# A third spread inflow (chunk 8) and six rows of C streamed through three tiles in a two-direction state-space kernel

## The reference

```
delta = softplus(dlt @ Wdt.T + bdt)              # per channel and token
for n in range(16):                              # N states of a channel
    h_n[t] = exp(delta[t] * A_n) * h_n[t-1] + delta[t] * B[t, n] * u[t]
y[t] = sum_n h_n[t] * C[t, n]  (+ u[t] * Dp)
```

## Time and profile before

| | us |
|---|---|
| median of 3 runs (lowest to highest) | 3288.13 (3287.22 to 3289.47) |
| the profiled execution | 3287.01 |
| its span, first to last instruction | 3285.2 |
| PE busy (share) | 2993.0 (91%) |
| DVE busy | 3017.2 (92%) |
| ACT busy | 2678.5 (82%) |
| POOL busy | 2903.7 (88%) |
| DMA moved | 560.40 MB, mean 171 GB/s |

### The profile page before, as it was taken

How to read it: one execution, slowest core, us unless ns; L and a number is a source line. 1 busy time by engine, 2 the same in 40 slices (tenths; PEclk the granted TensorE clock), 3 DMA queues, 4 the chain that set the end, 5 groups by cost and what they waited for, 6 DMA issues and landing times.

```text
span 3285.2 us, 54883 instructions
## 1 busy us (share of the span) xinstructions
PE 2993.0 (91%) x19924; PEld 2375.2 (72%) x19924; DVE 3017.2 (92%) x2008; ACT 2678.5 (82%) x5151; POOL 2903.7 (88%) x1288
## 2 busy tenths in 40 slices
PE   8887999899998999899999999899998999899999
PEld 5765666677677666678877767678777666677789
DVE  2838999999999999999999999999998999999994
ACT  1448999988888999987788999987877999988772
POOL 1528999999999999999999999999998999999993
PEclk9989999999999999999999999999999999999999
DMA  5775334644476333645465334645566343645463
GB/s 224 236 244 171 136 117 137 227 154 163 162 248 207 130 123 131 228 144 163 159 243 192 130 123 134 224 139 165 165 217 207 120 132 130 232 136 163 156 198 111
DMA packets 207053, 560.40 MB, mean 171 GB/s; under 512 B 20200, under 2 KB 66472, under 8 KB 202560
## 3 DMA queue, kind: packets, MB, share of 16 engines
q1 hardware_dynamic: 203424, 538.01, 48.5%
q0 software_dynamic: 2304, 16.78, 1.3%
q10 hardware_dynamic: 1056, 2.10, 0.2%
HBM read 476.19 MB, written 80.63 MB: 169 GB/s over the span
## 4 chain that ended last, share of the span: by engine, by line
PE 49%; ACT 20%; DVE 12%; issue 10%; POOL 1%; DVEq 0%; ACTq 0%; POOLq 0%
PE y L888 14%; PE slot L899 10%; PE mb L859 9%; ACT abuf L1134 8%; PE mb L969 6%; DVE hbuf L1326 6%; ACT slot L1195 3%; DVE hbuf L1335 3%; PE mb L869 3%; PE slot L911 3%; DVE slot L1326 3%; ACT dec L1195 2%; PE mb L930 1%; ACT soft L1090 1%; ACT yrd L1125 1%
## 5 line engine op out<-in xcount | busy, mean ns | idle before, releaser
L1239 POOL TENSOR_TENSOR hbuf<-hbuf,cres 128x1024 f32<-128x1024 f32 x704 | 1664.4, 2377 | 143.9 <-DVE hbuf L1326 143.8
L1234 POOL TENSOR_TENSOR bst<-bst,du 128x1024 f32<-128x1024 f32 x512 | 1220.2, 2383 | 46.7 <-DVE du L1270 46.7
L1326 DVE TENSOR_TENSOR_SCAN hbuf<-dec,slot 128x1024 f32<-128x1024 f32 x512 | 1165.0, 2275 | 40.3 <-PE slot L911 27.2
L888 PE MATMUL y<-ident,hbuf 128*128 128x128 f32 x8192 | 1016.0, 273 | 1.8 <-POOL hbuf L1239 1.7
L888 PEld LDWEIGHTS y<-ident,hbuf 128*128 128x128 f32 x8192 | 923.9, 141 | 106.4 <-issue 103.5
L1134 ACT ACTIVATE abuf<-dut,bt 128x128 f32<-128x128 f32 x3072 | 964.7, 387 | 0.0
L1326 DVE TENSOR_TENSOR_SCAN slot<-slot,bst 128x1024 f32<-128x1024 f32 x320 | 728.3, 2276 | 22.5 <-ACT slot L1195 22.1
L1195 ACT ACTIVATE slot<-delta,par 128x1024 f32<-128x1024 f32 x512 | 568.4, 1110 | 199.6 <-DVE hbuf L1335 186.6
L1195 ACT ACTIVATE dec<-delta,par 128x1024 f32<-128x1024 f32 x512 | 584.2, 1141 | 118.7 <-DVE hbuf L1326 118.1
L899 PE MATMUL slot<-ident,abuf 128*128 128x128 f32 x3072 | 408.6, 276 | 170.8 <-ACT abuf L1134 160.1
L899 PEld LDWEIGHTS slot<-ident,abuf 128*128 128x128 f32 x3072 | 339.0, 141 | 303.4 <-ACT abuf L1134 243.0
(11 more groups left out here) (157 smaller groups left out, 2301.3 us busy)
## 6 DMA issues: line engine op xcount, KB each, us to landing
bst<-bc_s SPq DMA_DIRECT2D x512, 512.0 KB, 3.9
cres<-bc_s SPq DMA_DIRECT2D x128, 512.0 KB, 6.8
wzs<-wz_s SPq DMA_DIRECT2D x64, 256.0 KB, 4.0
yf_s<-yrd SPq DMA_DIRECT2D x32, 512.0 KB, 5.3
ybuf<-yf_s SPq DMA_DIRECT2D x32, 512.0 KB, 4.8
yg_s<-ybuf SPq DMA_DIRECT2D x31, 512.0 KB, 4.4
si_s<-silu SPq DMA_DIRECT2D x28, 512.0 KB, 6.1
silu<-si_s SPq DMA_DIRECT2D x28, 512.0 KB, 5.4
```

What stands on the lines that cost most here:

```text
L888: last = nc.tensor.matmul(y[:, j * P:(j + 1) * P], hbuf[:, q % HR, j * P:(j + 1) * P], ident[:], start=False, stop=(q % N == N - 1), is_tr ...
L1234: nc.gpsimd.tensor_tensor(bst[:, i % BR, :], bst[:, i % BR, :], du[:, k % 2, :], ALU.mult).then_inc(pool_b, 1)
L1239: nc.gpsimd.tensor_tensor(hbuf[:, q % HR, :], hbuf[:, q % HR, :], cres[:, q % N, :], ALU.mult).then_inc(pool_prod, 1)
L1326: nc.vector.tensor_tensor_scan(h[:, ::step], decays[:, ::step], inflows[:, ::step], 0.0, ALU.mult, ALU.add).then_inc(scanned, 1)
```

## The change

`KINDS[8]` goes from A to E: chunk 8 becomes spread. Its two `scale_half` calls (chunks 6 and 7) go; the two of chunk 10 move from chunks 8 and 9 to 7 and 8. A third set of diagonals is made: before the first unit, and at chunk 3 of the first unit of every later group. `cres` shrinks from 16 tiles to 13: ten rows of C stay loaded for a group, and the six of `STREAMED` go through a ring of three tiles and are loaded anew in every unit, each when the product three streamed rows before it is done. `dec` gets a ring size, which is 1.

```diff
-KINDS = "EVAVEVAPAVAPAPAV"
-SCALE_STEPS = {0: ((2, 0), (2, 1)), 3: ((6, 0),), 5: ((6, 1),), 6: ((8, 0),), 7: ((8, 1),), 8: ((10, 0),),
-               9: ((10, 1),), 10: ((12, 0),), 11: ((12, 1),), 12: ((14, 0),), 13: ((14, 1),)}
+KINDS = "EVAVEVAPEVAPAPAV"
+SCALE_STEPS = {0: ((2, 0), (2, 1)), 3: ((6, 0),), 5: ((6, 1),), 7: ((10, 0),), 8: ((10, 1),),
+               10: ((12, 0),), 11: ((12, 1),), 12: ((14, 0),), 13: ((14, 1),)}
...
+STREAMED = (0, 3, 5, 8, 11, 13)
+KEPT = [n for n in range(N) if n not in STREAMED]
+CR = 3
+DECS = 1
...
+STREAM = [q for q in range(NU * N) if q % N in STREAMED]
...
-        cres = sb("cres", [P, N, S])
+        cres = sb("cres", [P, len(KEPT) + CR, S])
...
+            def load_streamed(i):
+                q = STREAM[i]
+                g = q // SEQ
+                sp.dma_start(cres[:, len(KEPT) + i % CR, :],
+                             scratch["bc"][g % 2, g // 2, N + q % N, :].partition_broadcast(P)).then_inc(cs_in[i % CR], 16)
...
-            for n in range(3):
+            load_streamed(0)
+            for n in (1, 2):
                 load_c(0, n)
+            for i in range(1, CR):
+                load_streamed(i)
...
                         load_b(before("VP", q - 2) + BR)
-                    if k == 0 and c + 3 < N:
+                    if k == 0 and c + 3 in KEPT:
                         load_c(0, c + 3)
+                    if q >= 5 and (q - 5) % N in STREAMED and stream_index(q - 5) + CR < len(STREAM):
+                        wait_product(sp, q - 5)
+                        load_streamed(stream_index(q - 5) + CR)
...
-                        wait_product(sp, q - ET)
+                        wait_product(sp, N * k + KEPT[c - ET])
...
-                    if e == ET - 1 and k + 1 < NU and c >= 5:
+                    if e == ET - 1 and k + 1 < NU and c - 5 in KEPT:
                         wait_product(sp, q - 5)
                         load_c(k // ET + 1, c - 5)
-                    if e == 0 and k >= ET and c < 5:
+                    if e == 0 and k >= ET and c < 5 and N - 5 + c in KEPT:
                         wait_product(sp, q - 5)
                         load_c(k // ET, N - 5 + c)
...
             make_diagonal(0, 1)
+            make_diagonal(0, 2)
...
-                        if before("AE", q) > 0:
-                            act.wait_ge(scanned, TURNED[before("AE", q) - 1] + 1)
-                        decays = dec[:]
+                        if before("AE", q) >= DECS:
+                            act.wait_ge(scanned, TURNED[before("AE", q) - DECS] + 1)
+                        decays = dec[:, before("AE", q) % DECS, :]
...
-                    if c == 1 and k > 0 and k % ET == 0:
-                        make_diagonal(k // ET, 1)
+                    if c in (1, 3) and k > 0 and k % ET == 0:
+                        make_diagonal(k // ET, (c + 1) // 2)
```

More of the change, by code:

```diff
@@ L537, in ssm_kernel @@
         delta, du = (sb(n, [P, 2, S]) for n in ("delta", "du"))
-        soft, ud, yrd, silu, ybuf, dec, dut = (sb(n, [P, S]) for n in (
-            "soft", "ud", "yrd", "silu", "ybuf", "dec", "dut"))
+        soft, ud, yrd, silu, ybuf, dut = (sb(n, [P, S]) for n in (
+            "soft", "ud", "yrd", "silu", "ybuf", "dut"))
+        dec = sb("dec", [P, DECS, S])
         abuf = sb("abuf", [P, 2, S])
@@ L554, in ssm_kernel @@
         c_in = [sem(f"c_in{n}") for n in range(N)]
+        cs_in = [sem(f"cs_in{i}") for i in range(CR)]
         last_in = sem("last_in")
@@ L617, in z_bank, with stream_index, c_tile, wait_c @@
             return mb[h] if k > 0 else y[:, half(h)]
+        def stream_index(q):
+            return q // N * len(STREAMED) + STREAMED.index(q % N)
+        def c_tile(q):
+            if q % N in STREAMED:
+                return cres[:, len(KEPT) + stream_index(q) % CR, :]
+            return cres[:, KEPT.index(q % N), :]
+        def wait_c(eng, q):
+            if q % N in STREAMED:
+                eng.wait_ge(cs_in[stream_index(q) % CR], 16 * (stream_index(q) // CR + 1))
+            else:
+                eng.wait_ge(c_in[q % N], 16 * (q // SEQ + 1))
         def wait_scanned_out(eng, q):
@@ L694, in load_c @@
             def load_c(g, n):
-                sp.dma_start(cres[:, n, :],
+                sp.dma_start(cres[:, KEPT.index(n), :],
                              scratch["bc"][g % 2, g // 2, N + n, :].partition_broadcast(P)).then_inc(c_in[n], 16)
+            def load_streamed(i):
[3 more added lines that the diff above has]
+                             scratch["bc"][g % 2, g // 2, N + q % N, :].partition_broadcast(P)).then_inc(cs_in[i % CR], 16)
             def load_forward_y(k):
@@ L1236, in product @@
             def product(q):
-                pool.wait_ge(c_in[q % N], 16 * (q // SEQ + 1))
+                wait_c(pool, q)
                 pool.wait_ge(scanned, q + 1)
-                nc.gpsimd.tensor_tensor(hbuf[:, q % HR, :], hbuf[:, q % HR, :], cres[:, q % N, :],
+                nc.gpsimd.tensor_tensor(hbuf[:, q % HR, :], hbuf[:, q % HR, :], c_tile(q),
                                         ALU.mult).then_inc(pool_prod, 1)
@@ L1318, in _ @@
                         dve.wait_ge(turned, before("AE", q + 1))
-                        decays, inflows = dec, slot[q % 2]
+                        decays, inflows = dec[:, before("AE", q) % DECS, :], slot[q % 2]
                     else:
@@ L1333, in _ @@
                         dve.wait_ge(scanned, q + 1)
-                        dve.wait_ge(c_in[c], 16 * (q // SEQ + 1))
-                        nc.vector.tensor_tensor(hbuf[:, q % HR, :], slot[q % 2][:], cres[:, c, :],
+                        wait_c(dve, q)
+                        nc.vector.tensor_tensor(hbuf[:, q % HR, :], slot[q % 2][:], c_tile(q),
                                                 ALU.mult).then_inc(dve_prod, 1)
```

## The result

The changed kernel takes **3366.20 us** (median of four runs, 3361.04 to 3372.34), against 3287.68 (3284.75 to 3289.47) for the kernel before on the same chip: a ratio of 1.0241, with a 95% interval of 1.0229 to 1.0253. The forecast was 3349 us, slower; the sign and the range hold, and the size is 17 us short. The profiled execution is 3369.61 us, 82.6 us above that of before.

What follows compares the result with a forecast made beforehand. DVE was taken as the bound nearly everywhere, with PE a second bound in series in silu units. Terms 26 + 2 + 10 + 22 = 60 us on 3287.0 gave 3347, as a median about 3349 us; range 3317 to 3379.

Steps and rivals of the forecast that it cites:

- the spread, PE later in 32 silu units: Chunk 8's spread makes PE 0.82 us later; DVE waits 0.8 us at the next chunk 0: 26 us.
- diagonals at seven group starts: At chunk 3 of seven later units the set delays decays: 3 x 2.0 + 4 x 1.0 = 10 us.
- before the first scan and in the first unit: Before the first unit the set of diagonals stands straight before the decay DVE awaits: 2.4 us.
- streamed row ahead of the tile: At chunk 13 of gate units with a block the tile lands 1.25 us later, DVE loses 0.9: 22 us.
- gate units without a projection, the tail: PE pauses in gate units take up most of the spread's delay; tail loads are used late: both 0.
- The wait at chunk 5: At group starts DVE waits 2 us for the decay of chunk 5; a sign to show in the profile after.
- the rival of the lower clock level: Tile waits about 1.9 us more, or the projection runs at lower clock after PE's pause: 3390 us, chance 0.07.
- The rows themselves: The six streamed rows of C arrive in time for their products; no POOL or DVE wait: 0.
- The clock: Rival that replacing eight transposes with true matmuls raises PE's clock, gaining 27 us: 3322 us, chance 0.02.
- ACT's relief: Removing ACT's scaling of chunk 8, some 2.5 us of a unit, gains 0.

Runs made afterwards that it cites:

- the half spread: Changed kernel with only four of the eight blocks of chunk 8's inflow made: 3334.33 us, ratio 1.0147.
- moving the set: Changed kernel with the third set of diagonals of later groups made at chunk 6 instead of chunk 3: 3349.51 us, ratio 1.0189.
- the z shift: Kernel before with the next unit's projection z in parts of 3, 2, 2, 1 instead of 2, 2, 2, 2, except in gate units: 3283.94 us, 0.9992.
- the streamed rows alone: Changed kernel with chunk 8 turned again and two sets of diagonals, the six streamed rows kept: 3320.55 us, ratio 1.0104.
- one streamed row: Kernel before with only row 8 of C loaded anew per unit, at step 13 directly ahead of the projection's tile: 3318.83 us, ratio 1.0095.
- the split: Kernel before with the next chunk 0's spread put behind 16 of the projection's 32 matmuls in gate units: 3286.97 us, ratio 1.0001.
- the order turned: Changed kernel with the streamed row issued last in its step, behind the unit's own loads: 3329.71 us, ratio 1.0134.

## Why the prediction was right, point by point

| step | forecast | measured |
|---|---|---|
| the spread, PE later in 32 silu units | 26 | 26 (28 units 22.9, and some 0.8 in each of the four group starts) |
| diagonals at seven group starts | 10 | 10 (4 x 1.0 and 3 x 2.0) |
| before the first scan and in the first unit | 2.4 | 5.5 (2.3 of it the set of diagonals) |
| streamed row ahead of the tile | 22 | 41 (32.0 and 3.5, and some 5 of the three starts) |
| gate units without a projection, the tail | 0 | 0.4 |
| sum | 60 | 82.6 |

**The spread.** Right in mechanism and size, 0.82 forecast and 0.81 measured, and the half spread takes the whole of it away. The place was right for three quarters of it: 0.62 us are lost behind chunk 8, nearly all at the scan of chunk 0, where the profile could name no releaser for most of it. The other 0.19 are lost at the scan of chunk 8, where the forecast had put the end of the spread (414.37) beside the start of the scan (414.35) and saw nothing lost; it had counted the 0.1 us of reaction ahead of the spread but not the same behind it. That does not change the sum, since time that DVE loses at chunk 8 is no longer lost at chunk 0.

**The diagonals.** Right in both: 1.1 and 2.2 us where I took 1 and 2. The wait at chunk 5 was there, and moving the set removed it.

**The tile of the projection.** The mechanism was right, and it is the term of the sum that was mis-sized. I took "the second lands 6.1 - 5.3 = 0.8 us later after its own issue". That is the price of a second transfer, and the tile became the third. Measured are 6.5 against 5.5, in unit 26 and at the median of 23, so 1.0 us, and with 0.47 of issue the tile is 1.5 us later instead of 1.25. Its lead over the projection was 0.3 us in unit 26, not 0.35, and the projection itself takes 0.07 us more. That makes 1.27 us in this unit and 1.38 at the median, not 0.9: some 31 us over 23 units, where I had taken 22. Unit 31 and three more (46, 58, 61) lost 2.2 to 2.8 us beyond that, together the other 10. In unit 58, with the window of the projection:

```profile
3060.20 5.33 PE L1005 MATMUL mb<-ybuf,wf 128*128 128x128 f32 x32 [2.42 <-issue]
...
3060.20:3065.53 5.33, 5.33 (x34) 5.33 (x35) 2.44 (x2) 3.62 (x10) 5.33 (x3) 0.70 0.93 336
```

The projection takes 5.33 us instead of 3.8, at a mean grant of 0.70, after a pause of 2.42 us. That is the rival of the lower clock level, which I had put in "half of 22 units" at 3.7 us each. It came in four, at 1.5 to 1.7 us of longer projection beside the longer wait. That these four fell to it and the others did not was not forecast. A fifth, k = 47, had it in the kernel before already:

```profile
2474.68 6.54 PE L969 MATMUL mb<-ybuf,wf 128*128 128x128 f32 x32 [4.07 <-issue]
```

**The start.** The first scan starts 4.9 us later, against 2.4 for a set of diagonals. DVE's wait ahead of it tells the two parts apart:

```profile
260.28 2.29 DVE L1363 TENSOR_TENSOR_SCAN hbuf<-dec,slot 128x1024 f32<-128x1024 f32 x1 [7.08 <-ACT dec L1232]
```

It is 7.08 us instead of 4.75, so the set costs 2.33 us, as forecast. It is 7.08 in every kernel here that makes the third set there, and 4.75 in every one that does not. The other 2.5 us are lost earlier, in a setup whose length scatters: without a third set the scans start 3.4 us later in the kernel with the z shift on before, 0.3 later with the streamed rows alone, and 1.2 earlier with one streamed row.

**The rows themselves.** In time, as forecast: neither POOL nor DVE has a wait for a transfer of C, which land in 5.7 us at the median and 13.0 at worst, against 6.5 and 12.5 before.

**The clock.** Over the 24 silu units with k mod 16 from 1 to 6 the granted clock has a mean of 0.99 in both kernels. In single ones it is 1.00 or 0.96, both before and after. The Trainium skill, "TensorE: Matmul & The Clock Gate", Part 4, has it that the full clock does not engage for transposes, which do not count as busy in the same way. The trace does not agree: in this stretch of the kernel before, 13 us long, TensorE runs 88 transposes and nothing else, with two pauses of over 1 us, at a grant of 1.00.

```profile
1555.73:1568.85 13.12, 10.06 (x88) 9.27 (x87) 13.12 (x9) 12.46 (x25) 10.73 (x6) 1.00 0.31 105
```

Eight transposes replaced with matmuls in each unit did not raise the clock either, though at a mean of 0.99 there was little to raise. Gate units with a projection fell from 1.00 to 0.99 in the mean: six of the 18 are at 0.96 or 0.97, which are 46, 58 and 61 with their slow projections, and 25, 41 and 57, whose projections took 3.81 us. Why these last three fell is not shown.

**ACT's relief.** Worth nothing, as forecast: 130 us less of work (some 150 forecast) and no wait shorter.

**What I had not seen.** That PE's run in a silu unit is tied to DVE and ACT in its middle. For the forecast it did not matter, because a later PE is late at every one of those places. For the way back it did: on the kernel before, neither the z shift nor the split gained anything. And that a row of B was already issued directly ahead of the tile, so that the kernel before did show a pair in that place, landing 5.5 us after the tile's issue.

## What to carry to other kernels

When a load lands only a few tenths of a microsecond ahead of its reader, as the tile did here, the place of any new transfer in that queue is worth more than its bytes: issue it behind the load. An engine that is relieved gives nothing unless somebody waits for it at that place, while the engine that takes over the work is charged in full if it has no pause from there to its next hand-over. And an added delay spread through this chain of two engines that arrive together (0.81 us a unit), but an equal gain did not (ratio 0.9992); price the two directions separately.

## What the runs showed of the hardware

A second transfer of 512 KB issued directly ahead of one of the same size made that one land 1.0 us later after its own issue (6.4 or 6.5 against 5.5 us at the median of 23), with the DMA engines 0.68 busy in the unit shown. With the same 736.64 MB but the order turned the median was 6.0 us and few waits were left. In the changed kernel pauses of 0.9 to 1.67 us ahead of the projection (18 units) left it at 3.81 us, and pauses of 1.96 to 4.74 us (five) were followed by 5.29 to 5.76 us. And over 13 us with transposes alone the granted clock stayed at 1.00.
